# A gated delta rule with its key norms moved out of the keys

## What is computed

```python
mixed = silu(causal_conv1d(hidden @ w_qkv, conv_w))     # 4 taps per channel
q, k, v = split(mixed)                                  # 16 key heads, 32 value heads, 128 wide
q = q * rsqrt(sum(q * q) + eps)
k = k * rsqrt(sum(k * k) + eps)                         # per token
beta, g = sigmoid(hidden @ w_b), -exp(A_log) * softplus(hidden @ w_a + dt_bias)
def step(St, q_t, k_t, v_t, g_t, b_t):                  # token after token
    St = St * exp(g_t)
    delta = (v_t - k_t @ St) * b_t
    St = St + outer(k_t, delta)
    return St, q_t @ St
out = (core * rsqrt(mean(core * core) + eps) * norm_weight * silu(hidden @ w_z)) @ w_out
```

## Time and profile before

| | before |
|---|---|
| median of 3 runs | 3313.22 us (3309.28 to 3315.47) |
| profiled execution, its span | 3310.8 us |
| PE busy | 3215.4 us, 97% |
| DVE busy | 2448.0 us, 74% |
| POOL busy | 1859.5 us, 56% |
| ACT busy | 1550.6 us, 47% |

### The profile page before, as it was taken

The page is one execution under the profiler, slowest core; times in us unless marked ns, Lnnn a source line. Parts: engine busy times, 40 slices in busy tenths (PEclk is TensorE's granted clock), DMA queues, the critical chain, the costliest instruction groups (busy, mean ns, idle before and its releaser), DMA issues. The chain is left out here.

```text
span 3310.8 us, 60236 instructions
## 1 busy us (share of the span) xinstructions
PE 3215.4 (97%) x20576; PEld 2131.6 (64%) x20576; DVE 2448.0 (74%) x3686; ACT 1550.6 (47%) x4983; POOL 1859.5 (56%) x1824
## 2 busy tenths in 40 slices
PE   5899999999999999999999999999979999999999
PEld 2577777777777777777777777777754444454444
DVE  6899999999999999999999999999940011034453
ACT  2465656565656565556555655565531000022232
POOL 2677777777777777777777777777730000011132
PEclk8999999999999999999999999999999999999999
DMA  2133333323333233323333332333325222211001
GB/s 94 48 77 84 77 72 74 85 70 74 80 84 75 69 80 76 77 70 83 80 75 73 80 81 70 77 79 81 81 62 207 76 102 102 76 39 64 0 13 39
DMA packets 423119, 248.75 MB, mean 75 GB/s; under 512 B 306688, under 2 KB 372352, under 8 KB 417280
## 3 DMA queue, kind: packets, MB, share of 16 engines
q1 hardware_dynamic: 421520, 237.81, 27.5%
q10 hardware_dynamic: 1296, 7.08, 0.5%
HBM read 156.39 MB, written 71.57 MB: 69 GB/s over the span
## 5 line engine op out<-in xcount | busy, mean ns | idle before, releaser
L736 PE MATMUL acc<-xT,wc 128*128 128x512 f32 x2048 | 934.8, 599 | 2.7 <-PEq L112 2.0
L736 PEld LDWEIGHTS acc<-xT,wc 128*128 128x128 f32 x2048 | 369.7, 190 | 372.6 <-issue 372.0
L1015 DVE SCALAR_TENSOR_TENSOR d_conv<-acc,wc,d_conv 128x511 f32<-128x511 f32 (+2 forms) x768 | 566.8, 738 | 41.8 <-ACT d_conv L1190 32.6
L749 PE MATMUL acc<-wc,xT 128*128 128x256 f32 x2048 | 473.4, 384 | 0.0
L749 PEld LDWEIGHTS acc<-wc,xT 128*128 128x128 f32 x2048 | 379.1, 190 | 46.2
L1541 PE MATMUL acc<-t_area 128*128 128x512 f32 x768 | 332.5, 592 | 1.6 <-ACT t_area L1990 1.6
L634 POOL TENSOR_TENSOR d_bf<-d_kks,d_gam 128x512 f32<-128x512 f32 x128 | 160.6, 1277 | 294.9 <-ACT d_kks L1234 294.9
L2047 POOL TENSOR_SCALAR t_veps<-t_mv 128x1 f32<-128x1 f32 x32 | 9.7, 303 | 547.0 <-DVE t_mv L1786 547.0
L1048 DVE STREAM_TRANSPOSE d_em<-d_dm 128x1024 f16<-128x1024 f16 x256 | 314.5, 1228 | 2.2
L1776 DVE TENSOR_TENSOR t_x<-acc,t_x 128x512 f32<-128x512 f32 x16 | 11.1, 691 | 392.3 <-PE acc L1541 392.3
L1055 DVE TENSOR_TENSOR d_zm<-d_tz,cons 128x512 f16<-128x512 f32 x384 | 259.0, 674 | 52.0 <-PE d_tz L799 47.0
(11 more groups left out here) (228 smaller groups left out, 7002.3 us busy)
## 6 DMA issues: line engine op xcount, KB each, us to landing
d_decay<-decay_rows SPq DMA_DIRECT2D x64, 512.0 KB, 5.2
v_rows<-d_vb SPq DMA_DIRECT2D x256, 128.0 KB, 2.3
d_vn<-v_rows SPq DMA_DIRECT2D x64, 512.0 KB, 3.7
core_rows<-d_ob SPq DMA_DIRECT2D x1024, 32.0 KB, 1.7
t_area<-core_rows SPq DMA_DIRECT2D x30, 1024.0 KB, 4.8
wc<-in_w SPq DMA_DIRECT2D x96, 256.0 KB, 3.2
d_qn<-d_qf SPq DMA_DIRECT2D x1024, 16.0 KB, 1.8
t_x<-in_x SPq DMA_DIRECT2D x4, 1024.0 KB, 9.2
```

What stands on the lines that cost most here:

```text
L736: last = nc.tensor.matmul(bank(TILE[j])[:, :], wtile(j, k), xT[:, k, r % B * S:(r % B + 1) * S], start=k == 0, stop=k == KT - 1)
L749: last = nc.tensor.matmul(bank(f"z{j}")[:, i * GV * P:(i + 1) * GV * P].rearrange("p (h n) -> p h n", h=GV), xT[:, k, r % B * S + (2 * j + ...
L1015: nc.vector.scalar_tensor_tensor(c[:, d:S], bank(TILE[j])[:, 0:S - d], tap(j, KS - 1 - d), c[:, d:S], ALU.mult, ALU.add).then_inc(taps, 1)
```

## The change

In every product the raw activated keys stand in `kT`, which the silu now writes directly, and `khat_turn` and `copy_kT` are gone. With N the norm of a token's key, the kernel now works with values times N and with raw keys over N squared, which leaves the state as it was. So POOL computes two factors per token in one power instruction (`rk`, now 128x2x4, exponents -1 and 0.5). The factor -1 goes into `normal_k`, and into the copies of `kk` and `kq` out of PSUM, which become four copies of one chunk each, with a scale per partition. The factor 0.5 goes into a new function `scale_v`, four ACT instructions of 128x256 in place on `vn`, which stand ahead of `copy_d(s, 5, 0)`. The core of the diff:

```diff
-        RING_ORDER = ("q", "k", "z1", "v1", "k_turn", "z0", "kq", "v0", "khat_turn", "kk")
+        RING_ORDER = ("q", "k", "z1", "v1", "k_turn", "z0", "kq", "v0", "kk")
...
             def k_norm(n):
                 pool.wait_ge(k_squares, at(n, NC, NC))
                 nc.gpsimd.tensor_tensor(rkt[:, :], kss[:, :], cons[:, C_L2:C_L2 + NC], ALU.add).then_inc(rk_ready, 1)
                 pool.wait_ge(rk_ready, at(n, 2, 1))
-                wait(pool, khat_ready, at(back(n, 1), NC, NC))
-                nc.gpsimd.tensor_tensor(rk[:, :], rkt[:, :], cons[:, C_POW:C_POW + NC], ALU.pow).then_inc(rk_ready, 1)
+                wait(pool, kqs_ready, at(back(n, 2), NC, NC))
+                wait(pool, v_scaled, at(back(n, 2), NC, NC))
+                nc.gpsimd.tensor_tensor(rk[n[1] % 2][:, :, :], bc(rkt[:, :], 2), cons[:, C_KPOW:C_KPOW + 2 * NC].rearrange("p (e c) -> p e c", e=2),
+                                        ALU.pow).then_inc(rk_ready, 1)
...
-                turn(bank("k_turn"), kraw, k_turned)
-
-            def khat_turn(n):
-                pe.wait_ge(khat_ready, at(n, NC, NC))
-                ring_free(n, "khat_turn")
-                turn(bank("khat_turn"), khat[n[1] % 2], khat_turned)
+                turn(bank("k_turn"), kT[third(n)], k_turned)
...
             def kk(n):
-                pe.wait_ge(kT_ready, count(n))
+                pe.wait_ge(silued, nth(n, "silued", 0))
...
-                    pe.wait_ge(v_moved, at(s, 80, 80))
+                    pe.wait_ge(v_scaled, at(s, NC, NC))
...
-                if project:
-                    khat_turn(n)
...
                 if j == 0:
-                    wait(act, k_turned, count(n, 1))
+                    wait(act, ks_s, at(back(n, 3), 3, 3))
...
-            def copy_kT(n):
-                act.wait_ge(khat_turned, count(n))
-                nc.scalar.activation(kT[third(n)][:, :], bank("khat_turn")[:, :], ACT.Copy).then_inc(kT_ready, 1)
+            def scale_v(s):
+                act.wait_ge(v_moved, at(s, 80, 80))
+                for c in range(NC):
+                    v = vn[s[1] % 2][:, :, :, :].rearrange("p a (h c) j -> p (a h) c j", c=NC)[:, :, c, :]
+                    nc.scalar.activation(v, v, ACT.Copy, scale=rk[s[1] % 2][:, 1, c:c + 1]).then_inc(v_scaled, 1)
...
-                nc.scalar.activation(kks[:, :], bank("kk")[:, :], ACT.Copy).then_inc(kk_copied, 1)
+                for c in range(NC):
+                    nc.scalar.activation(chunk(kks, c), chunk(bank("kk"), c), ACT.Copy, scale=rk[n[1] % 2][:, 0, c:c + 1]).then_inc(kk_copied, 1)
...
                 if recur:
+                    scale_v(s)
                     copy_d(s, 5, 0)
...
-                if project:
-                    copy_kT(n)
```

More of the change, by code:

```diff
@@ L45 @@
 C_RMS = C_L2 + NC
-C_END = C_RMS + NC
+C_KPOW = C_RMS + NC
+C_END = C_KPOW + 2 * NC
 DECW = S
@@ L68, in shape_constants @@
     c[:, C_RMS:C_RMS + NC] = L2_EPS * RMS_EPS * HD
+    c[:, C_KPOW:C_KPOW + NC] = -1.0
+    c[:, C_KPOW + NC:C_KPOW + 2 * NC] = 0.5
     for h in range(XH):
@@ L323, in delta_rule @@
         cb, decay, ident = many("conv", 2, [P, S]), sb("decay", [P, GV, S]), sb("ident", [P, S])
-        kraw, vraw, vn = sb("kraw", [P, S]), sb("vraw", [P, GV, S]), many("vn", 2, [P, NC, GV * NC, 32])
+        vraw, vn = sb("vraw", [P, GV, S]), many("vn", 2, [P, NC, GV * NC, 32])
         khat = many("khat", 2, [P, S])
@@ L340, in delta_rule @@
         junk, kqs, kks = sb("junk", [P, 3 * NC, P], BF16), sb("kqs", [P, S]), sb("kks", [P, S])
-        kss, qss, rkt, rk = sb("kss", [P, NC]), sb("qss", [P, NC]), sb("rkt", [P, NC]), sb("rk", [P, NC])
+        kss, qss, rkt, rk = sb("kss", [P, NC]), sb("qss", [P, NC]), sb("rkt", [P, NC]), many("rk", 2, [P, 2, NC])
         qf, qn = sb("qf", [P, NC, NC, 32]), sb("qn", [P, NC, NC, 32])
@@ L354, in delta_rule @@
         k_turned, k_squares, rk_ready = sem("k_turned"), sem("k_squares"), sem("rk_ready")
-        khat_ready, khat_turned, kT_ready, ks_ready = sem("khat_ready"), sem("khat_turned"), sem("kT_ready"), sem("ks_ready")
+        khat_ready, ks_ready, v_scaled = sem("khat_ready"), sem("ks_ready"), sem("v_scaled")
         q_moved, q_squares, eq_ready = sem("q_moved"), sem("q_squares"), sem("eq_ready")
@@ L430, in per_token @@
             return bc(ap, P, 2)
-        RING_ORDER = ("q", "k", "z1", "v1", "k_turn", "z0", "kq", "v0", "khat_turn", "kk")
-        RING_BANK = {"q": 1, "k": 2, "z1": 0, "v1": 1, "k_turn": 2, "z0": 0, "kq": 2, "v0": 0, "khat_turn": 2, "kk": 1}
+        RING_ORDER = ("q", "k", "z1", "v1", "k_turn", "z0", "kq", "v0", "kk")
+        RING_BANK = {"q": 1, "k": 2, "z1": 0, "v1": 1, "k_turn": 2, "z0": 0, "kq": 2, "v0": 0, "kk": 1}
         RING_FREED = {"k": (taps, "taps", 2), "q": (taps, "taps", 5), "v0": (taps, "taps", 8), "v1": (taps, "taps", 11),
                       "z0": (z_silued, "z_silued", 0), "z1": (z_silued, "z_silued", 1),
-                      "k_turn": (khat_ready, "squares", NC - 1), "khat_turn": (kT_ready, "once", 0),
-                      "kk": (kk_copied, "once", 0), "kq": (kqs_ready, "once", 0)}
+                      "k_turn": (khat_ready, "squares", NC - 1),
+                      "kk": (kk_copied, "squares", NC - 1), "kq": (kqs_ready, "squares", NC - 1)}
         CONV_ORDER = ("k", "v1", "v0", "q")
@@ L448, in delta_rule @@
                     "zr_ready": (1, 2), "closed": (2, 1), "tt_ready": (2, 1)}
-        RING_LAG = {"q": 1, "k": 0, "z1": 2, "v1": 0, "k_turn": 0, "z0": 2, "kq": 1, "v0": 0, "khat_turn": 0, "kk": 0}
+        RING_LAG = {"q": 1, "k": 0, "z1": 2, "v1": 0, "k_turn": 0, "z0": 2, "kq": 1, "v0": 0, "kk": 0}
         CONV_LAG = {"k": 0, "v1": 0, "v0": 0, "q": 0}
@@ L630, in b_full @@
             def b_full(n, h):
-                pool.wait_ge(kk_copied, count(n))
+                pool.wait_ge(kk_copied, at(n, NC, NC))
                 pool.wait_ge(gams_ready, nth(n, "gams_ready", h))
@@ L636, in p_full @@
             def p_full(m, h):
-                pool.wait_ge(kqs_ready, count(m))
+                pool.wait_ge(kqs_ready, at(m, NC, NC))
                 pool.wait_ge(gamc_ready, nth(m, "gamc_ready", h))
@@ L779, in kq @@
             def kq(m):
-                pe.wait_ge(kT_ready, count(m))
                 pe.wait_ge(silued, nth(m, "silued", 1))
@@ L1198, in silu @@
                 v = vraw
-                out = (kraw[:, :], qT[third(n)][:, :], v[:, 0, :], v[:, 1, :])[j]
+                out = (kT[third(n)][:, :], qT[third(n)][:, :], v[:, 0, :], v[:, 1, :])[j]
                 nc.scalar.activation(out, conv_of(TILE[j])[:, :], ACT.Silu).then_inc(silued, 1)
@@ L1246, in normal_k @@
                 for c in range(NC):
-                    nc.scalar.activation(chunk(khat[n[1] % 2], c), chunk(bank("k_turn"), c), ACT.Copy, scale=rk[:, c:c + 1]).then_inc(khat_ready, 1)
+                    nc.scalar.activation(chunk(khat[n[1] % 2], c), chunk(bank("k_turn"), c), ACT.Copy, scale=rk[n[1] % 2][:, 0, c:c + 1]).then_inc(khat_ready, 1)
             def copy_kq(m):
@@ L1251, in copy_kq @@
                 wait(act, p_ready, at(back(m, 1), GV, GV))
-                nc.scalar.activation(kqs[:, :], bank("kq")[:, :], ACT.Copy).then_inc(kqs_ready, 1)
+                for c in range(NC):
+                    nc.scalar.activation(chunk(kqs, c), chunk(bank("kq"), c), ACT.Copy, scale=rk[m[1] % 2][:, 0, c:c + 1]).then_inc(kqs_ready, 1)
             def copy_d(m, l, n):
```

## The result

The changed kernel takes 3329.9 us (median of 4 runs, 3327.9 to 3331.6), the kernel before beside it 3313.9 us (4 runs, 3309.3 to 3315.5): a ratio of 1.005, with a 95% interval from 1.0036 to 1.0064. It is slower by 15.9 us. The profiled execution has a span of 3326.1 us against 3310.8 us.

The account below looks back on a forecast made before the run. It took PE and an equally long PE-DVE-PE path to bound the stretch losing the transposes. 0 + 17.6 - 1.5 = +16.1 us on 3313.2 gave 3329.3 us; 8-in-10 range 3314 to 3338.

Parts of the forecast that it names:

- The four transposes at 0: PE between level_d(m, 2) and read_k(s, 2): dropping 0.48 us a slot gains 0, as DVE's path is as long.
- the prediction's sign of being right: Plain slots stay at 36.5 us; PE waits for DVE 0.4 us in sum in each stretch after level_d(m, 2).
- Rival 1: Faster: PE gets the transposes' time back, 30.7 us in all, giving 3298.6 us; chance 0.12.
- `scale_v`: Four ACT copies ahead of copy_d(s, 5, 0): fit in plain slots, hold PE 1.17 us in 15 slots with new weights.
- T: Time of the four scale_v copies on ACT, taken as 1.6 us, bounds 1.2 and 2.7 us.
- the slack of 0.43: Slots with new weights: PE's refine(s, 0) starts 0.43 us after copy_d's end and the 0.06 us semaphore.
- Its size, 17.6 us: Loss from scale_v: 15 slots x 1.17 us = +17.6 us, bounds +11.6 and +34.
- the wait of 4.8 us: ACT's first tap in a slot with new weights waits 4.8 us for the transfer, making all behind it late.
- The power of eight values, 0, with 0.21 us left: POOL's rk comes 0.63 us later; price 0, with 0.21 us left before ACT's copy of z.
- Rival 3: Slower still: the power takes 2.2 us, delaying the copy of z and first state, 11.5 us: 3341 us; chance 0.06.
- The split copies, 0: ACT's copy_kq and copy_kk get about 0.5 us longer each, covered by waits and an earlier kk; price 0.
- The first slot, -1.5: PE's query projection in the first slot starts at 86.5 instead of 87.99; gain 1.5 us, once.

Follow-up runs that it names:

- Experiment 4: Experiment 1's kernel with four transposes of the keys put back at khat_turn's place, result unused: 3304.6 us, ratio 0.9978 to the kernel before.
- experiment 9: DVE's scan behind the convolution taps and attend(s, 1) ahead of read_k(s, 2): 3292.1 us in experiment 1's kernel, 3302.7 us in the kernel before, key turn kept.
- experiment 1: Changed kernel with scale_v moved behind copy_d(s, 5, 0) on ACT: 3313.5 us, ratio 1.0003 to the kernel before.
- experiment 2: Kernel before with only four in-place ACT copies of vn, factor one, added at scale_v's place: 3331.1 us, ratio 1.0056.
- experiment 3: Changed kernel with a second set of four copies of the values, factor one, behind the first: 3407.0 us, ratio 1.028.
- experiment 5: Experiment 1's kernel with DVE's scan of head 1's decays put behind the three convolution taps of the queries: 3300.4 us, ratio 0.9959.
- experiment 6: DVE's scan of head 1's decays put behind the three query taps: 3301.8 us in the kernel before, 3302.5 us in the changed kernel as it stands.
- experiment 8: Experiment 1's kernel with attend(s, 1) moved ahead of read_k(s, 2) and four unused key transposes put back: 3326.4 us, ratio 1.0038.

## Why the prediction was right

It forecast 3329.3 us, with the profile's span 2.4 us under the median, and 3329.9 us were measured. By its steps:

*The four transposes at 0.* Right, and by the mechanism named: the stretch is 3.54 us against 3.55, DVE's four steps are unchanged, PE waits for `d_state` 64 times, and its small waits in the stretch add up to the 0.48 us, as the prediction's sign of being right had it (0.4). Experiment 4 adds them again for nothing. Rival 1 (3298.6 us) is refuted: PE was at 97%, and 64 x 0.48 us of its work were worth nothing. The Trainium skill's advice to improve the engine with the highest occupancy ("Perfetto Trace Analysis", Identifying the Most-Contended Engine) would have given that rival if the busy share of matmuls is taken for occupancy, against which the same section warns; so taken, this case goes against it until experiment 9 fills the gap.

*`scale_v`.* T was estimated at 1.6 us; four take 1.70 us to the last end, and `copy_d` is late by 1.98 - 0.38 = 1.60. The hold ahead of `refine` is 1.17 us, as worked out from the slack of 0.43. Experiments 1 and 2 show that this place alone makes the loss, and experiment 3, in its plain slots, that the room of 2.22 and 0.43 us is what counts.

*Its size, 17.6 us.* A little small: the 15 slots are longer by 19.5 us, 1.30 each. 1.17 is the hold. The rest is, by the timelines, the taps' later arrival: against PE's work the first tap comes 0.13 us later in the slots shown, because the scan in front takes 2.27 us and not 2.04, and PE's wait ahead of `attend(f, 2)` grows by just that, from 0.36 to 0.49 us (0.16 us in the mean of the 15). The prediction looked for idle time of PE behind `refine` alone; this one lies ahead of it and was not priced. The prediction took the wait of 4.8 us as a fixed thing of the transfer. It is a wait for DVE, and so for POOL; it was the step that was not looked into, and the one with the larger gain behind it (experiments 5 and 6).

*The power of eight values, 0, with 0.21 us left.* Right. POOL and ACT in a plain slot after, which answer to the earlier trace rows:

```profile
1022.31 1.64 POOL L598 TENSOR_TENSOR d_rk<-d_rkt,cons 128x8 f32<-128x8 f32 x1
...
1024.03 1.14 ACT L1247 ACTIVATE d_khat<-acc,d_rk 128x128 f32<-128x128 f32 x4 [0.94 <-issue]
1025.38 0.60 ACT L1202 ACTIVATE d_sz<-acc 128x512 f32<-128x512 f32 x1 [0.20 <-PE acc L754]
```

ACT still waits 0.20 us for PE's z behind the copies into `khat`. Rival 3 is out.

*The split copies, 0.* Not contradicted: experiment 6 puts all that the change does outside the late place at 0.7 us, within the scatter.

*The first slot, -1.5.* Right at its place: PE needs 6.31 us from `k_turn` to the query projection (rows below, PE's timeline), where it took 7.83 (from 80.16 to 87.99). But the next slots gave 1.2 us back, and at the first `solve(s, 0)`, 56 us after `k_turn`, 0.3 us are left. The term should have been near 0.

```profile
77.23 0.66 PE L761 MATMUL acc<-cons,d_kT 128*128 128x128 f32 x4 [2.70 <-ACT d_kT L1197]
...
83.54 6.68 PE L741 MATMUL acc<-xT,wc 128*128 128x512 f32 x15 [1.32 <-ACT d_kks L1234]
```

The slots' measured sum, 19.4 us, is more than the 15.9 us between the medians, and more than the 17.6 of the forecast. The 3.5 us between are not explained; they are of the size by which the part ahead of the slots scatters from profile to profile (2.6 us at the first projection already). One term was too small by 2 us and another gave 1.5 us that did not last. That the forecast came within 1 us is therefore in part luck.

## What to carry to other kernels

Work taken from the busiest engine is worth nothing while another engine's path of the same length runs beside it: look at what ends at the next common point, and if work is taken out there, bring other work of the same engine into the gap in the same edit. Price an inserted instruction by the least room that its place ever has, in the rare slots too: 1.6 us were free in 48 slots and cost 1.2 us in each of 15. And where a rare slot waits for a transfer, read what the transfer waited for, before taking its length as given.

## What the runs showed of the hardware

- The same VectorE scan (two SBUF operands, 128x512) takes between 1.21 and 2.29 us in the changed kernel (up to 2.35 in that of experiment 8), by what GpSimd does beside it, and GpSimd's product beside it 1.15 or 2.08 us. A shift of GpSimd by 0.28 us decided between 2.27 and 1.32 us, and with it some 9 us of the kernel (experiment 4).
- An idle time of TensorE of 2.59 us cost 1.68 us more in the slot shown, by a granted clock of 0.50 afterwards. It did so in 12 slots of 15, at different prices, and in three not at all (experiment 3). Idle times of 1.00 us, with a shorter one ahead, cost none in the 15 slots of the changed kernel and did in one of the 15 of experiment 2.
- Four 128x256 copies with a per-partition scale on ScalarE take 1.70 us, a start every 0.40 us in the mean (a second set began 1.60 us after the first).
